# In layer 0, VectorE subtracts the maximum from the fourth pair of scores; GpSimd keeps the other three

## The reference, cut to what matters

```
attn = einsum(q * scale, k) + relative_position_bias + mask
attn = softmax(attn, axis=-1)          # exp(attn - max) / sum
out  = einsum(attn, v) @ proj_w + proj_b
```

## Time and profile before

| what | value |
|---|---|
| median of 3 runs | 7809.69 us (7807.17 to 7815.15) |
| the profiled execution's own time | 7816.85 us |
| its span | 7815.1 us |
| busy, share of the span | PE 94%, DVE 78%, POOL 68%, ACT 63% |
| costliest POOL groups | subtraction L654: 2059.0 us, x2048; masks L644: 683.2 us, x515 |
| costliest ACT wait | exponential L777 on POOL's L654: 809.2 us |

### The profile page before, as it was taken

The page is one execution under the profiler, slowest core; times in us unless marked ns, Lnnn a source line. Parts: engine busy times, 40 slices in busy tenths (PEclk is TensorE's granted clock), DMA queues, the critical chain, the costliest instruction groups (busy, mean ns, idle before and its releaser), DMA issues.

```text
span 7815.1 us, 310674 instructions
## 1 busy us (share of the span) xinstructions
PE 7327.9 (94%) x109686; PEld 5700.3 (73%) x109686; DVE 6100.8 (78%) x18297; ACT 4899.6 (63%) x8745; POOL 5299.8 (68%) x6555
## 2 busy tenths in 40 slices
PE   5999999999899999999989999999999999999998
PEld 3777777777677777777767777777776777777777
DVE  6878878777786887877878687786787778778677
ACT  3746647557674765746767475574677647567467
POOL 4956657567795765757789476674778857567576
PEclk9999999999999999999999999999999999999999
DMA  2101101010110110101011011010101101011010
GB/s 62 39 11 30 52 12 33 11 36 17 25 40 30 35 47 17 33 7 43 10 31 51 19 34 43 22 33 7 45 4 37 57 11 33 14 27 30 11 42 25
DMA packets 309909, 227.60 MB, mean 29 GB/s; under 512 B 217379, under 2 KB 305766, under 8 KB 306344
## 3 DMA queue, kind: packets, MB, share of 16 engines
q1 hardware_dynamic: 307858, 215.98, 10.3%
q10 hardware_dynamic: 1622, 6.13, 0.2%
HBM read 117.62 MB, written 104.37 MB: 28 GB/s over the span
## 4 chain that ended last, share of the span: by engine, by line
POOL 35%; issue 27%; PE 22%; DVE 7%; POOLq 4%; DVEq 2%; ACT 1%; ACTq 0%
POOL S L654 17%; PE ps L1082 8%; PE ps L1055 7%; POOL G L644 7%; POOL xn L670 4%; POOL rstd L626 4%; DVE xn L1257 2%; DVE bst L1108 2%; PE ps L1069 2%; DVE x L1419 1%; PE ps L901 1%; DVEq L1257 1%; POOL mv L697 1%; PE ps L932 1%; POOLq L476 1%
## 5 line engine op out<-in xcount | busy, mean ns | idle before, releaser
L654 POOL TENSOR_TENSOR S<-S,mx 113x588 f32<-113x588 f32 (+1 forms) x2048 | 2059.0, 1009 | 896.3 <-DVE mx L1299 878.2
L777 ACT ACTIVATE S<-S 113x588 f32<-113x588 f32 (+1 forms) x2048 | 1246.9, 609 | 823.9 <-POOL S L654 809.2
L959 PE MATMUL ps<-turn,S 113*123 113x113 f32 (+2 forms) x8704 | 1329.2, 278 | 103.7 <-ACT PT L782 73.7
L1299 DVE TENSOR_REDUCE mx<-S 113x12 f32<-113x588 f32 (+1 forms) x2048 | 1359.4, 664 | 70.6
L782 ACT ACTIVATE PT<-ps 123x490 f32<-123x490 f32 (+1 forms) x2048 | 1051.1, 513 | 458.7 <-PE ps L959 438.6
L959 PEld LDWEIGHTS ps<-turn,S 113*123 113x123 f32 (+2 forms) x8704 | 927.7, 167 | 514.9 <-ACT PT L782 328.9
L1055 PEld LDWEIGHTS ps<-w,G 128*98 128x98 f32 x12288 | 1150.5, 167 | 159.3 <-issue 87.6
L1055 PE MATMUL ps<-w,G 128*98 128x96 f32 (+1 forms) x12288 | 1151.3, 250 | 0.0
L1082 PE MATMUL ps<-h,w 97*128 97x392 f32 x3072 | 1124.1, 502 | 9.1 <-ACT G L865 9.1
L1296 DVE TENSOR_TENSOR S<-ps,bias 113x588 f32<-113x588 f32 (+1 forms) x1536 | 963.9, 628 | 181.9 <-PE ps L948 135.2
L932 PEld LDWEIGHTS ps<-Va,PT 123*49 123x49 f32 (+1 forms) x18432 | 755.8, 125 | 326.3 <-ACT PT L782 255.0
(11 more groups left out here) (94 smaller groups left out, 12145.3 us busy)
## 6 DMA issues: line engine op xcount, KB each, us to landing
v_between<-Vd SPq DMA_DIRECT2D x384, 165.4 KB
Va<-v_between SPq DMA_DIRECT2D x768, 41.3 KB
Vb<-v_between SPq DMA_DIRECT2D x768, 27.6 KB
v_between<-Vd SPq DMA_DIRECT2D x128, 153.1 KB
Vl<-v_between SPq DMA_DIRECT2D x256, 76.6 KB
out_dram<-x SPq DMA_DIRECT2D x15, 1176.0 KB
x<-x_dram SPq DMA_DIRECT2D x14, 1176.0 KB
mask<-mask_dram SPq DMA_DIRECT2D x258, 37.5 KB
```

Source lines behind the costliest of these rows:

```text
L654: pool.tensor_tensor(v, v, m, ALU.subtract).then_inc(a_sub, 1)
L777: act.activation(S[:, p, 0:nh * N], S[:, p, 0:nh * N], ACT.Exp).then_inc(a_exp, 1)
L959: last = pe.transpose(ps[0:rows, PT_BANK, PAIR * b:PAIR * b + TOK], S[:, p, at:at + rows], turn[:, :])
L1299: dve.reduce_max(mx[:, s, 0:nh], S[:, s, 0:n].rearrange("p (h k) -> p h k", k=N), axis=AX.X).then_inc(a_mx, 1)
```

## The change

In layer 0, POOL leaves out sub3 of every step, and DVE makes it right after m3. DVE waits ahead of it for sub2 of the same step (`a_sub`), so that the semaphore that ACT counts rises in order, and for its own m3. Layers 1 to 3 are as before.

```diff
@@ gpsimd, attend @@
                         if s == 3 and on(0):
                             below(2)
-                            below(3)
+                            if l > 0:
+                                below(3)
@@ vector, attend @@
                         if s == 3 and on(0):
                             bias_and_max(3)
+                            if l == 0:
+                                wait(a_sub, i.pair(2))
+                                wait(a_mx, i.pair(3))
+                                v = S[:, 3, 0:n].rearrange("p (h k) -> p h k", k=N)
+                                m = mx[:, 3, 0:nh].unsqueeze(2).to_broadcast([TOK, nh, N])
+                                dve.tensor_tensor(v, v, m, ALU.subtract).then_inc(a_sub, 1)
```

## The result

The changed kernel took 7881.91 us (median of 4 runs, 7877.45 to 7885.37) against 7809.81 us (4 runs, 7807.17 to 7815.15). It is slower by 72 us; 112 us were forecast, and the time lies inside the range, near its lower end. A second set of 4 runs gave 7884.78 us, 1.0094 [1.0079, 1.0110].

What follows compares the result with a forecast made beforehand. POOL was the largest engine, its relief limited by PE's 10.25 us step. POOL's 8.80 plus 2.59 for DVE and m0 to sub0 made 11.39 us against 10.485: +0.905 x 124 = +112 us, 7922 us; range 7870 to 7980.

Steps and rivals of the forecast that it cites:

- the ring: Layer 0's step: POOL's sub0 to M2', then DVE's sub3, aggregate, b0, m0, then next sub0; 11.39 us a step.
- Rival 2: Layer 0's steps: DVE's waits for PE stay, 12.20 us a step, +213 us, 8022; chance 0.08.
- sub3's tail: On DVE in layer 0: sub3 ends 0.66 us after POOL's M2', bounds 0.02 and 0.76 plus 0.06.
- It fixes an order: Layer 0: DVE's wait for sub2 lets POOL start M2' first, so sub3 always meets a running M2'.
- rival 3: Layer 0: DVE comes late to sub3, only part of M2' is in the way, 10.36 to 10.61 us; chance 0.04.
- PE and the rest can do a step in 10.25 us: Floor for layer 0's step, taken from layer 1; POOL's relief can bring 0.233 us a step, at most some 29 us.
- rival 1: Layer 0: no collision, or sub3 runs ahead of M2'; 10.24 us, PE's 10.25 decides, 29 us less, 7781; chance 0.08.
- The first of rival 2's two terms: Layer 0: with both PE waits staying, m2 is 0.30 us late when POOL reaches sub2; taken as nothing.
- The other marks: Changed profile: sub3 about 1.9 us, ending 0.6 to 0.7 after M2'; POOL idle 2.6 before sub0; masks 1.34; layers 1-3 unchanged.

Runs made afterwards that it cites:

- no_sub3: The changed kernel with pair 3's subtraction left out in layer 0; DVE only signals the semaphore after the same waits: 7810.81 us, 0.9997.
- relief_only: The kernel before without pair 3's subtraction in layer 0 on either engine; the exponential waits for m3, DVE has no added wait: 7796.40 us, 0.9980.
- mask_after_sub3: The changed kernel with POOL's last mask of a step (M2') waiting for DVE's sub3: 7812.58 us, 0.9997.
- late_aggregate: As mask_after_sub3, and in layer 0 DVE makes the aggregate after m0 of the next step, not ahead of b0: 7780.63 us, 0.9965.
- load_two_inputs: The kernel before plus an unused DVE subtraction of two SBUF blocks behind m3 in 104 steps of layer 0: 7833.53 us, 1.0030.
- late_aggregate_alone: The kernel before with only layer 0's aggregate moved behind m0, subtractions all on POOL: 7815.28 us, 1.0004.
- the two loads: The kernel before plus an unused DVE instruction behind m3 in 104 layer 0 steps: one SBUF input 7813.55 us, two 7833.53 us.
- no_wait_for_sub2: The changed kernel without DVE's wait for sub2; sub3 raises its own semaphore, which ACT's exponential of pair 3 waits for: 7890.04 us, 1.0098.

## Why the prediction was right, and where it wasn't

**The direction and the mechanism were right.** The new subtraction is held up beside M2', and the hold closes the ring sub0 to M2', sub3, aggregate, b0, m0. Four runs show it from four sides: no hold with M2' moved away, no hold with one input, a hold on the other engine when DVE comes first, and, with M2' ahead of sub2, a ring as long without any hold. Rival 2 (12.20 us a step) didn't occur.

**The size was too large: 72 us instead of 112.** A steady step rose by 0.71 us instead of 0.905. The ring measured, from the timelines above: POOL from 300.32 to the end of M2' at 309.06, 8.74 (8.80 forecast); sub3's tail 0.64 (0.66); the next start 0.08 ahead of its recorded end (0.09); aggregate to b0 309.90 - 309.62 = 0.28 (0.37 was taken, the recorded duration, not start to start); b0 to m0 0.77 (0.80); m0 to sub0 0.85 (0.85). The sum is 11.20 us against 11.39. Nearly every term was a little too long, the aggregate's by most: 0.19 x 124 = 24 us. Of the remaining 88 us the stages lost 81. The rest is in their first steps, where the ring isn't closed yet: in the first group the first takes 9.57 us in both kernels, the second 10.77 instead of 10.33, the third 10.91 instead of 10.82, which is 1.6 us less than three steady ones would lose, or some 6 in four groups. Of the 81 us 64 are left between the two profiled executions and 72 between the medians. So everything outside these stages came out 9 to 17 us shorter, a term that the prediction didn't have; the last section shows a part of it.

**"It fixes an order" wasn't what decided.** sub3 always meets a running M2', as the prediction said, but without the wait for sub2, which was to make it so, the step is 11.205 us. What binds is m3, which ends 0.16 us after sub2 in the changed kernel. With this the argument against rival 3 falls, that sub3's start hangs on M2' and not on DVE. That the wait itself costs little was right: sub2 ends ahead of m3 in no_sub3 as well. What the prediction left out is DVE's stop behind m3 for its own m3 and the raise, about 0.25 us a step where no hold covers it (no_sub3 against relief_only).

**"PE and the rest can do a step in 10.25 us" failed for layer 0.** relief_only reaches 10.37, so in the step 0.115 us were to be gained, not 0.233; its medians differ by 18 us, not 29. With this rival 1's price falls too: without a hold the change costs 10.62 us a step, not 10.24, and the time is that of the kernel before. The relief is eaten, as far as the runs show, because the aggregate, and b0 and m0 with it, come later: they start 0.8 us behind m3's end in mask_after_sub3 (309.59 to 310.39), and in relief_only 0.09 ahead of it. late_aggregate, which takes the aggregate's 0.37 us out from between, supports that with 10.457 us. Which chain through ACT and PE makes up the 10.62 us was not isolated.

**Waits.** DVE's waits ahead of b0 and the reciprocal went, as forecast (0.2 us in the window is left of b0's 13.8). The one ahead of `Vd` stayed: 11.9 / 26 = 0.46 us a step. It cost nothing, though by little: m2 starts at 316.89, and 0.85 later, as from m0 to sub0, sub2 may start, at 317.74. By its own list POOL comes to it at 311.52 + 6.29 = 317.81 (from sub0 to sub2 as in the step above), 0.07 us later. The first of rival 2's two terms stayed away by no more than that.

**The other marks** came as said: POOL idles 2.45 us ahead of sub0 (2.6), the masks keep 1.32 to 1.34 us, the attention stages of layers 1 to 3 are unchanged (by less than 1 us over four groups). Layer 2's MLP stage isn't (last section). The new instruction took 1.65 us, not 1.9, since it is recorded from m3's end and not from sub2's; its end, which counts, was 0.64 us after M2' in the step shown, and 0.62 to 0.64 in all 124 steps with a mask. All 128 of them, the line over the whole trace (min/median/max ns):

```profile
L1352 DVE TENSOR_TENSOR S<-S,mx x128: 770/1647/1736, 118.4 to 6296.4; 113x588 f32<-113x588 f32 x128
```

In the first group's step 31, where no mask follows, it took 0.77 us, recorded from 466.86, beside the end of a root on POOL.

The Trainium skill, page "Perfetto Trace Analysis", section "Optimizing Scalar/DVE Operations", warns that offloading between GpSimd and VectorE might not help, as they share a port. Here it made 7810 into 7882 us, and with the port out of the way (mask_after_sub3) it still brought nothing.

## What to carry to other kernels

Before an elementwise operation goes from POOL to DVE, count its SBUF inputs and look at what POOL executes just then: here, with two inputs, it waited for a running POOL instruction, and the profile shows that as DVE busy time. Then draw the ring that the move closes across both engines, and add it up start to start, not with recorded durations. If the ring is longer than the old step, move what isn't needed there to where nobody waits for it (here a mask into POOL's idle time, and an aggregate behind m0). And look at the step before the total: here a step that was 0.14 us longer stood behind an equal time.

## What had not been expected of the hardware

**The hold goes both ways, by who is first.** The prediction's rows, and the figures expected for load_two_inputs, had only DVE waiting. There a DVE instruction that started 0.16 us ahead made POOL's subtraction 1.63 us long instead of 1.17. In the earlier trace rows DVE waited through four POOL instructions in a row; here, in the ring, it waited for one, and POOL had nothing to run behind it until m0 was done.

**A stage that the edit doesn't touch changed its speed.** The stretch from a layer-2 attention stage to that of layer 3 was shorter than before by 5.9 and 7.0 us (four stretches together) in the two profiles of the changed kernel and by 5.4 to 10.9 us in the six other kernels with an edit behind m3 in every step of layer 0, though the lists of layer 2 are those of before; in relief_only, late_aggregate_alone and the two loads it was longer by 0.1 to 1.8 us. The traces show where: in layer 2's MLP stage. ACT's line that occurs once in each of its steps, in a window of the first group, before and after:

```profile
L865 ACT ACTIVATE G<-ps x21: 1151/1151/1152, 1475.9 to 1571.6; 128x1176 f32<-128x1176 f32 x21
...
L866 ACT ACTIVATE G<-ps x21: 1150/1150/1152, 1491.8 to 1585.4; 128x1176 f32<-128x1176 f32 x21
```

A step takes 95.7 / 20 = 4.785 us before and 93.6 / 20 = 4.680 after. The eight profiles with the shorter stretch all have 4.68, the others 4.78 to 4.80. In every second step DVE stands ahead of one instruction, with nothing in the profile that it waits for, 0.69 us before and 0.58 after, and the instruction is 0.1 us longer before:

```profile
1505.62 1.49 DVE L1257 TENSOR_SCALAR xn<-x,mv,rstd 98x96 f32 x4 [0.69 <-issue]
...
1520.73 1.39 DVE L1258 TENSOR_SCALAR xn<-x,mv,rstd 98x96 f32 x4 [0.58 <-issue]
```

Layer 0's MLP steps fall into two such groups as well (4.72 to 4.75 us, and 4.78 to 4.80), but there the two loads are with the faster ones and no_wait_for_sub2 is with the slower. The end of layer 0's attention is less steady still: from the last `Vd` to the first L865 the kernel before takes 27.6 to 32.6 us from group to group, late_aggregate 26.4 to 27.5. Each kernel but the changed one has a single profile, and no run separated a cause, so it stays open. It is why 0.2% between two such kernels should not be put down to the edited step without a look at the step itself.
